# First feed-forward: its two square layers as seven products of quarters over two token blocks at a time

## The chip, the cores and the metric

The program runs on one core of one Trainium2 chip. The metric is the device time of one execution in microseconds. The kernel before took 2341.57 us, the median of three runs (2340.15 to 2347.95).

## The reference

Input is `x`, 4 sequences of 1024 tokens with 256 features, all in float32. Four parts follow one another, each behind a layer norm and added to `x`:

1. an attention with 8 heads of 64 and a latent of 64 for keys and values;
2. a feed-forward with ternary weights (-1, 0 or 1) and a scale per output:
```
h = silu(tlin(x, w1)) * tlin(x, w2)      # 256 -> 1024
h = gelu(tlin(h, h1))                    # 1024 -> 1024
h = gelu(tlin(h, h2))                    # 1024 -> 1024
y = tlin(h, w3)                          # 1024 -> 256;  tlin(x, w) = (x @ w.T) * s
```
3. an attention with 16 heads of 16 and rotated queries and keys;
4. a gated feed-forward of width 768 with integer weights.

The change is in part 2, and in what parts 1 and 3 do for it or beside it.

## The kernel before, in words

**Two programs.** `attention_a` is part 1, `ffn_attention_ffn` holds parts 2 to 4. Each engine has its own function (`sync`, `scalar`, `vector`, `gpsimd`, `tensor`), whose order is written out by hand: every engine walks the same numbered slots and does in each what the slot's functions name. Engines meet through semaphores alone, so an instruction that waits holds back all that its engine has behind it. All DMAs are issued by SyncE.

**Part 1.** A turn (`u, j`) is two steps of 128 keys for a pair of heads; there are 128 turns. TensorE makes scores, maxima twelve steps ahead, and weighted values; ScalarE the exponents (L631) and half of the maxima's work (L598); VectorE the other half (L785) and some sums of exponents (L803, L807); GpSimd the other sums (L952 to L959). Beside that, one weight tile of part 2 every four turns (`tile_at`, `load_tile` L523 to L529) is copied in DRAM to `wcopy`, loaded to `tile`, rounded by ScalarE (`tile_high`, L687) and compared by VectorE (L831). If no tile changes by the rounding, a flag lets the later program multiply rounded operands in one pass each (`exact`), with an activation as a high part and a low part that are multiplied one after the other.

**Part 2.** 4096 tokens are 8 blocks of 512 (`NB`). A block has 64 slots (`SLOTS`), and its 352 matmuls of 128x128 weights on 128x512 activations are spread over them, five or six in a slot (`slice_at`, `tile_of`): 64 for gate and up, 128 for each of the two square layers, 32 for down. An output tile of the square layers is 16 matmuls into one PSUM bank (8 inner pieces, high and low). Six banks go round (`Y`, `y_order`). Weights stream from `wcopy` through three buffers `wt`, one tile of 512 KB for 16 matmuls (L1594 to L1598). ScalarE applies Gelu twice per tile, once to the rounded high part and once to `xf` (L1874, L1875); GpSimd subtracts them to make the low part (`low`, L2070). For the gated layer ScalarE makes Silu, VectorE multiplies (`up`, L2012), ScalarE rounds (L1860), GpSimd subtracts.

**Side work.** One PSUM bank `X` serves, slot by slot (`x_at`), what stands beside the products. For block k it is done in the slots of block k+1: four transposes back with the residual (`BACK`), then the norm for part 3 on VectorE (`C_STATS` slot 15, `C_SCALE` slot 18, L184 to L206), two turns to feature order (`C_TURN` slots 22 and 24: TensorE transposes, ScalarE copies, VectorE subtracts, L227, L238, L249), four projections of queries and keys (`PROJECT`, each followed by three GpSimd operations of rotation, L2078 to L2082, and a low part, L2087) and four of values. The norm for the next block's gated layer (`B_STATS` to `B_TURN`) comes after. TensorE can begin a side operation only when the bank's user before it has been read out (`wait_free`). In the slots of each engine the side operation stands first, then the read-out of finished tiles, then the norm:

```
for H in range(END):
    if maximum_at(H) is not None: reduce(maximum_at(H))
    x = x_at(H) or ("",)
    ...                                  # turn, swap, residual
    for key in ended_at(H):
        if key[0] == "up": up(key)
    ...
    if norm_at(H): norm_step(*norm_at(H))
```

**Part 3** begins at slot `START` = 512 and has 512 half-steps. Each has one exponent of 128x1024 on ScalarE (L1813) and one maximum of 128x1024 on VectorE (L1965); the first 24 maxima stand in the last 24 slots of part 2. The side work of block 7 lies in its first 45 slots. Queries go through three tiles for units 2 to 4 (a unit is 16 half-steps) and four from unit 5. **Part 4** follows at slot 1024.

## Time and profile before

| what | value |
|---|---|
| median of three runs | 2341.57 us (2340.15 to 2347.95) |
| the profiled execution | 2332.85 us |
| its span, first to last instruction | 2331.0 us |
| granted TensorE clock, mean | 0.996 |
| part 1 | from 0 to about 720 us |
| part 2 | 722.6 to 1460 us |
| part 3 | 1461 to about 2192 us |
| part 4 | to the end |

Times come from one profiled execution. Matmuls overlap, so that the duration of one (0.39 us) is not what it adds: how far apart they start is. A group's "idle before" names the time its engine stood still in front of it and what ended that. The stages are read apart, since another engine can be the full one in each.

### The profile page before, as it was taken

What the parts mean: (1) busy time and instruction counts of PE and PEld (TensorE: products, weight loads), DVE (VectorE), ACT (ScalarE), POOL (GpSimd) and SP (SyncE); (2) the same over time, 40 slices, a digit from 0 to 9 for tenths busy, and PEclk for the clock granted to TensorE, in tenths of its full rate; (3) what the DMA queues carried; (4) which work ended last, traced back from release to release, by engine and by line L of the source; (5) the groups of instructions that cost most, each with busy time, mean ns of one, the idle gap of its engine ahead of it and who ended that gap; (6) DMA issues with size and microseconds to landing.
All of it is one profiled execution on the core that took longest, in us unless ns stands there. A gap on an engine that the chain in (4) does not pass through costs nothing.

```text
span 2331.0 us, 39372 instructions
## 1 busy us (share of the span) xinstructions
PE 2286.6 (98%) x14921; PEld 1414.8 (61%) x14921; DVE 1378.5 (59%) x2150; ACT 1463.2 (63%) x2049; POOL 1001.8 (43%) x646
## 2 busy tenths in 40 slices
PE   7999999999998999999999999999999999999999
PEld 5455555555556888888888886444444444444688
DVE  6655766666743143232232224889889889998364
ACT  5777777777764444444444443678777777778643
POOL 2676766757763373664655645120100000000354
PEclk9999999999999999999999999999999999999999
DMA  2213222222214455555555546343332332331232
GB/s 63 69 52 100 82 74 84 82 80 76 74 31 165 158 178 183 183 182 192 182 175 190 193 165 190 92 105 77 90 87 59 93 82 64 92 90 41 81 112 77
DMA packets 156841, 259.07 MB, mean 111 GB/s; under 512 B 37004, under 2 KB 97292, under 8 KB 156300
## 3 DMA queue, kind: packets, MB, share of 16 engines
q1 hardware_dynamic: 156652, 256.53, 36.6%
q8 instruction: 121, 1.98, 0.4%
q14 instruction: 68, 0.56, 0.1%
HBM read 206.52 MB, written 60.68 MB: 115 GB/s over the span
## 4 chain that ended last, share of the span: by engine, by line
PE 63%; ACT 2%; DVE 1%; issue 1%; DMA 1%; SPq 1%; POOL 0%; POOLq 0%
PE m_R L130 47%; PE m_O L130 11%; PE m_X L130 4%; ACT m_P L1813 1%; DMA m_K<-bounce_k 1%; PE m_X L227 1%; SPq L1671 0%; DVE m_mraw L1965 0%; ACT m_OS L1820 0%; PE m_X L2179 0%; DVE m_ln_x L206 0%; PE m_R L227 0%; DMA inverses<-m_rinv 0%; DVE m_ln_stat L184 0%; SPq L1698 0%
## 5 line engine op out<-in xcount | busy, mean ns | idle before, releaser
L1965 DVE TENSOR_REDUCE m_mraw<-m_R 128x2 f32<-128x1024 f32 x512 | 622.6, 1221 | 68.5 <-PE m_R L130 56.0
L1813 ACT ACTIVATE m_P<-m_R 128x1024 f32<-128x1024 f32 x512 | 523.7, 1025 | 148.6 <-PE m_R L130 148.3
L130 PE MATMUL m_O<-m_P,m_V 128*17 128x256 f32 x4096 | 329.4, 393 | 4.4 <-ACT m_P L1813 2.5
L785 DVE CUSTOM_DVE_ANT_0 a_excess<-a_X,a_excess 128x512 f32<-128x512 f32 x256 | 166.5, 688 | 170.6 <-PE a_X L130 167.9
L955 POOL TENSOR_TENSOR a_accp<-a_accp,a_P 128x1024 f32<-128x1024 f32 x96 | 253.9, 2645 | 24.5 <-ACT a_P L631 16.2
L631 ACT ACTIVATE a_P<-a_S 128x1024 f32<-128x1024 f32 x256 | 249.7, 1040 | 8.5 <-PE a_S L130 8.5
L2070 POOL TENSOR_TENSOR m_act0l<-m_xf,m_act0h 128x512 fp32r<-128x512 f32 x128 | 164.8, 1290 | 209.2 <-ACT m_xf L1875 110.9
L130 PE MATMUL m_R<-m_act0h,wt 128*128 128x512 f32 x640 | 251.4, 393 | 0.0
L130 PE MATMUL m_R<-m_act0l,wt 128*128 128x512 f32 x640 | 250.4, 391 | 0.0
L130 PE MATMUL a_O<-a_P,a_V 128*64 128x512 f32 x1024 | 247.7, 605 | 0.0
L130 PE MATMUL m_R<-m_Q,m_K 64*128 64x512 f32 x800 | 200.1, 497 | 2.3 <-DVE m_mraw L1965 2.0
L130 PE MATMUL m_R<-m_act1l,wt 128*128 128x512 f32 x512 | 202.0, 395 | 0.0
L130 PE MATMUL m_R<-m_act1h,wt 128*128 128x512 f32 x512 | 200.7, 392 | 0.0
L130 PE MATMUL m_R<-m_K,m_Q 48*128 48x512 f32 x800 | 181.7, 449 | 3.8 <-ACT m_P L1813 1.9
L2094 POOL TENSOR_TENSOR m_ON<-m_ON,m_yt 128x512 f32<-128x512 f32 x16 | 20.6, 1285 | 380.1 <-DMA m_yt<-inverses 380.1
L130 PE MATMUL m_R<-next_hi,wt 128*128 128x512 f32 x424 | 168.1, 396 | 2.8 <-PEq L40 2.8
L130 PEld LDWEIGHTS m_O<-m_P,m_V 128*17 128x17 f32 x4096 | 85.2, 120 | 139.3 <-issue 129.8
L130 PE MATMUL m_R<-next_lo,wt 128*128 128x512 f32 x424 | 167.7, 395 | 0.0
L130 PEld LDWEIGHTS m_R<-m_Q,m_K 64*128 64x128 f32 x800 | 74.5, 183 | 150.9 <-issue 126.0
L598 ACT ACTIVATE a_excess<-a_X 128x512 f32<-128x512 f32 x244 | 132.2, 596 | 36.3 <-PE a_X L130 35.5
L130 PEld LDWEIGHTS m_R<-m_act0h,wt 128*128 128x128 f32 x640 | 120.2, 188 | 26.9 <-POOL m_act0l L2070 2.1
L130 PEld LDWEIGHTS m_R<-m_act0l,wt 128*128 128x128 f32 x640 | 120.3, 188 | 24.5 <-issue 0.5
(274 smaller groups left out, 4130.1 us busy)
## 6 DMA issues: line engine op xcount, KB each, us to landing
wt<-wcopy SPq DMA_DIRECT2D x176, 512.0 KB, 3.3
m_K<-bounce_k SPq DMA_DIRECT2D x96, 128.0 KB, 5.5
m_ln_x<-x SPq DMA_DIRECT2D x23, 512.0 KB, 4.0
a_tile<-in_L_ffn_tiles SPq DMA_DIRECT2D x22, 512.0 KB, 3.6
wcopy<-in_L_ffn_tiles SPq DMA_DIRECT2D x22, 512.0 KB, 5.0
x<-xres SPq DMA_DIRECT2D x78, 128.0 KB, 1.7
m_Q<-bounce_q SPq DMA_DIRECT2D x150, 64.0 KB, 2.3
xres<-x SPq DMA_DIRECT2D x64, 128.0 KB, 2.7
```

Source lines behind the costliest of these rows:

```text
L130: return pe.eng.matmul(out, lhsT, rhs, start=start, stop=stop, skip_group_check=True)
L227: ins = pe.eng.transpose(bank[:, 128 * k:128 * k + 128], self.x[:, 4 * half + k, 128 * f:128 * f + 128], ident)
L598: act.eng.activation(excess[:, h, :], max_bank(n, h), ACT.Relu).then_inc(freed)
L631: act.eng.activation(P[n % NP][:, :, :], psS[n % 2][:, :, :], ACT.Exp, scale=SCALE).then_inc(s_exp)
L785: dve.eng.tensor_tensor_reduce(excess[:, h, :], bank(key), excess[:, h, :], 1.0, LOWEST, ALU.add, ALU.max, mraw[u % 2][:, q, h:h + 1]).the ...
L955: pool.eng.tensor_tensor(accp[:, :, :], accp[:, :, :], P[n % NP][:, :, :], ALU.add).then_inc(s_addp)
L1813: act.eng.activation(P[h % 4][:, :, :], pair(key)[:, :, :], ACT.Exp, scale=SCALE).then_inc(R.free(key))
L1965: dve.eng.tensor_reduce(mraw[u % 2][:, at, :], pair(key)[:, :, :], AX.X, ALU.max).then_inc(R.free(key))
L2070: pool.eng.tensor_tensor(act_buf[dst][1][:, m, :], xf[fs(key) % 2][:, :], f32(act_buf[dst][0][:, m, :]), ALU.subtract).then_inc(s_lo)
L2094: pool.eng.tensor_tensor(ON[:, f, cols], ON[:, f, cols], yt[half][:, :], ALU.mult).then_inc(s_norm[half])
```

## The change

**Two blocks at a time.** Blocks 2s and 2s+1 form a pair of 128 slots with five matmuls in each (`PACE`), 640 in all: 128 gate and up, 224 for each square layer, 64 down. Input features are halved (4 pieces of 128 each), output features are halved, and the two token blocks are the other halving, so that a layer is a 2x2 by 2x2 product of quarters, done by seven products (`m1` to `m7`) of 4 output tiles x 4 inner pieces x 2 parts. `m1` and `m2` share their banks, as do `m5` and `m3`.

**Sums of weights.** Four of the seven need sums of weight quarters. They are made in part 1, in four sets (`MIXES`) of 18 turns: the set's four quarter tiles are loaded and compared as before, then come four sums or differences of 128x1024 on VectorE and four stores of 512 KB to `wcopy` (now 38 tiles). The stores stand two turns behind the instructions that make their data. One quarter in four needs no copy in DRAM. The rounded tile for the comparison is int8.

**Sums of activations.** For every layer and each of 4 pieces VectorE makes four sums or differences of 128x512 in place (`mix`, each waiting for the one before), in slots 23, 25, 26 and 28 of the pair for the first square layer and 67, 69, 70 and 72 for the second. VectorE adds product to product (`leave`); ScalarE keeps `m1`, applies Gelu once per tile, and rounds 28 operands per layer and 16 for down (`high`); the low parts go to GpSimd and VectorE (`by_pool`).

**Side work** moves one block later: block k's lies in the slots of block k+2 (even: norm statistics in slot 21 and scaling in 24, turns in 28 and 30; odd: 15, 18, 22, 24 of the second 64). So part 3 now begins with the side work of blocks 6 and 7. The norm of block 1 is made in slots 2 to 9 of the first pair. The first 24 maxima go from slot 456 on, one in two slots, in one buffer. Queries have three tiles up to unit 8. Fills of `K1`, `Q2` and `V` go to GpSimd at slot 502.

```diff
-    NB, MT, PER, SLOTS = 8, HID0 // 128, 22, 64
+    NB, MT, PER, SLOTS, PACE = 8, HID0 // 128, 40, 64, 5
...
+    FIRST_MAX = START - 2 * ML - 8
...
-    BACK = (2, 4, 6, 8)
-    C_LOAD, C_STATS, C_SCALE, C_TURN = 10, 15, 18, (22, 24)
+    ORDER = ("m1", "m2", "m6", "m7", "m4", "m5", "m3")
+    OPERAND = dict(zip(ORDER, ("b11", "b21", "t2", "t3", "t4", "t1", "b22")))
...
+    BACK = (6, 8, 10, 12, 14, 16, 18, 20)
+    C_LOAD, C_STATS, C_SCALE, C_TURN = (16, 10), (21, 15), (24, 18), ((28, 30), (22, 24))
+    PROJECT = [{at + i: x for at, x in ((0, ("k", 0)), (4, ("q", 0)), (8, ("k", 1)), (12, ("q", 1)))} for i in (32, 26)]
...
+    N_LOAD, N_STATS, N_SCALE, N_TURN = 51, 56, 60, (2, 4)
+    ONE_STATS, ONE_SCALE, ONE_TURN = 2, 4, (7, 9)
...
-    QUERY_TILES = [0, 1, 2, 0, 1] + [(3, 2, 0, 1)[(u - 5) % 4] for u in range(5, NU)]
+    QUERY_TILES = [0, 1, 2] * 3 + [(3, 0, 1, 2)[(u - 9) % 4] for u in range(9, NU)]
...
+        layer, r = divmod(q - 128, 224)
+        if layer < 2:
+            return (ORDER[r // 32], 2 * s + layer, r // 8 % 4), r % 8, 8
+        return ("down", 2 * s + r // 32, r // 16 % 2), r % 16, 16
...
+            if l % 2:
+                H = (640 * (l // 2) + 128 + 192 + 8 * j + 7) // PACE + 2
+            else:
+                H = high_slot(("b22", l, j)) + 2
```
The new part of part 1 on SyncE and VectorE:
```diff
+                elif step == 12:
+                    sp.wait_ge(s_mix, 4 * n + 3)
+                    sp.eng.dma_start(sum_of(n, 0), f32(tile_hi[:, :])).then_inc(s_mixed, 16)
+                    sp.eng.dma_start(sum_of(n, 2), tile[:, :]).then_inc(s_mixed, 16)
+                    sp.eng.dma_start(sum_of(n, 1), third).then_inc(s_mixed, 16)
+                elif step == 13:
+                    sp.wait_ge(s_mixed, 64 * n + 48)
+                    sp.eng.dma_start(tile[:, :], wtiles[quarter(n, 0, 1)]).then_inc(s_tile, 16)
...
+                if i == 0:
+                    dve.eng.tensor_tensor(second, first, second, ALU.add).then_inc(s_mix)
```
And of part 2 on ScalarE, VectorE and GpSimd:
```diff
+            def keep_first(key):
...
+                act.eng.activation(kept[m], psY[Y.slot(("c11", l, m))][:, :], ACT.Copy).then_inc(s_kept)
...
+            def high(op):
+
+                act.wait_ge(*made(op))
+                if operand_free(op):
+                    act.wait_ge(*operand_free(op))
+                act.eng.activation(operand(op)[0], in_place(op), ACT.Copy).then_inc(s_hi)
...
+                elif name == "m7":
+                    dve.wait_ge(*Y.emptied(("m6", l, m)))
+                    dve.eng.tensor_tensor(kept[m], bank, twos[m], ALU.add).then_inc(Y.free(key))
...
+            def mix(l, j):
+
+                x11, x12, x21, x22 = [whole[place][j] for place in ("11", "12", "21", "22")]
+                n = 4 * mix_order[l, j]
+                dve.wait_ge(*(gelu_done(l - 1, "12", j) if l % 2 else up_done(l, "12", j)))
+                dve.wait_ge(*low_done(("b22", l, j)))
+                dve.eng.tensor_tensor(x22, x22, x12, ALU.subtract).then_inc(s_mixed)
+                dve.wait_ge(s_mixed, n + 1)
+                dve.wait_ge(*low_done(("b11", l, j)))
+                dve.eng.tensor_tensor(x12, x12, x11, ALU.subtract).then_inc(s_mixed)
+                dve.wait_ge(s_mixed, n + 2)
+                dve.eng.tensor_tensor(x11, x22, x11, ALU.add).then_inc(s_mixed)
+                dve.wait_ge(s_mixed, n + 3)
+                dve.wait_ge(*low_done(("b21", l, j)))
+                dve.eng.tensor_tensor(x21, x21, x11, ALU.subtract).then_inc(s_mixed)
...
+                for op in lows_at(H, False):
+                    low(op)
+                for l, j in mixes_at(H):
+                    mix(l, j)
...
+                pool.eng.tensor_tensor(lo, in_place(op), f32(hi), ALU.subtract).then_inc(s_lo[1])
```
On TensorE `m2` waits for `keep_first` of its tile and adds to that bank:
```diff
+                    if key[0] == "m2":
+                        pe.wait_ge(s_kept, 4 * key[1] + key[2] + 1)
+                    elif key[0] == "m3":
+                        pe.wait_ge(s_c22, 4 * key[1] + key[2] + 1)
```

## Rows read from the trace of the kernel before

**Rows 1.** Page of the profile, busy time by engine over the span
```profile
PE 2286.6 (98%) x14921; PEld 1414.8 (61%) x14921; DVE 1378.5 (59%) x2150; ACT 1463.2 (63%) x2049; POOL 1001.8 (43%) x646
```

**Rows 2.** Stretches (start:end, length, busy us and count by engine): feed-forward, second attention, one block
```profile
722.60:1460.40 737.80, 737.25 (x3371) 598.68 (x3371) 219.41 (x399) 331.99 (x534) 403.36 (x318) 1.00 0.56 181
1461.00:2192.00 731.00, 719.30 (x6395) 308.58 (x6394) 632.03 (x636) 565.10 (x629) 66.18 (x64) 1.00 0.32 79
971.29:1062.56 91.27, 91.27 (x426) 75.62 (x425) 24.65 (x50) 42.18 (x69) 53.20 (x42) 1.00 0.57 184
```

**Rows 3.** Chain that ended last inside the feed-forward (880 to 1336 us): start, us, what
```profile
by line: PE m_R L130 88.1%; PE m_X L130 9.1%; PE m_X L227 1.8%; PE m_X L2179 1.0%
...
971.29 19.98 PE m_R L130 x88
```

**Rows 4.** Groups by line in the feed-forward stage (722 to 1460 us)
```profile
L130 PE MATMUL m_R<-m_act0h,wt 128*128 128x512 f32 x640 | 251.4, 393 | 0.0
...
L2070 POOL TENSOR_TENSOR m_act0l<-m_xf,m_act0h 128x512 fp32r<-128x512 f32 x128 | 164.8, 1290 | 209.2 <-ACT m_xf L1875 110.9 <-ACT m_act0h L1860 98.3
...
L1875 ACT ACTIVATE m_xf<-m_R,scol 128x512 f32<-128x512 f32 x128 | 87.3, 682 | 0.0
...
L1860 ACT ACTIVATE m_act0h<-m_xf 128x512 fp32r<-128x512 f32 x64 | 39.9, 623 | 4.3 <-DVE m_xf L2012 4.3
...
L2012 DVE SCALAR_TENSOR_TENSOR m_xf<-m_R,scol,m_P 128x512 f32<-128x512 f32 x32 | 24.0, 751 | 23.0 <-PE m_R L130 22.1
...
L249 DVE TENSOR_TENSOR next_lo<-m_X,next_hi 128x512 fp32r<-128x512 f32 x28 | 19.4, 692 | 149.6 <-ACT next_hi L238 149.6
```

**Rows 5.** Timeline of VectorE around one normalisation (start, us, instruction)
```profile
941.79 1.39 DVE L184 BATCH_NORM_STATS2 m_ln_stat<-m_ln_x 128x6 f32<-128x256 f32 x4
943.21 0.38 DVE L187 BATCH_NORM_AGGREGATE m_ln_mv<-m_ln_stat 128x2 f32<-128x6 f32 x4
943.63 0.85 DVE L192 TENSOR_SCALAR m_ln_ve<-m_ln_mv 128x4 f32<-128x4 f32 x1
...
949.33 5.27 DVE L206 TENSOR_SCALAR m_ln_x<-m_ln_x,m_ln_mv,m_ln_rstd 128x256 f32<-128x256 f32 x4 [0.34 <-POOL m_ln_rstd L201]
```

**Rows 6.** Timeline of VectorE, 740 to 749 us: differences of two SBUF tiles
```profile
741.10 1.45 DVE L1989 TENSOR_TENSOR m_wql<-m_P,m_wqh 128x512 fp32r<-128x512 f32 x1 [1.22 <-ACT m_wqh L1898]
742.47 0.68 DVE L1989 TENSOR_TENSOR m_wkl<-m_P,m_wkh 128x512 fp32r<-128x512 f32 x1
```

**Rows 7.** Line 206 over the whole span: ns min/median/max
```profile
L206 DVE TENSOR_SCALAR m_ln_x<-m_ln_x,m_ln_mv,m_ln_rstd x92: 397/412/1391, 768.3 to 2296.2; 128x256 f32<-128x256 f32 x92
```

**Rows 8.** Groups of VectorE in the first attention (0 to 722 us)
```profile
L803 DVE TENSOR_TENSOR a_accd<-a_P 128x1024 f32<-128x1024 f32 x32 | 61.8, 1931 | 0.4
L831 DVE SCALAR_TENSOR_TENSOR a_tile_hi<-a_tile,a_tile_hi 128x1024 f32<-128x1024 f32 x27 | 56.9, 2109 | 0.0
```

**Rows 9.** Line 803, the same operation, ns min/median/max
```profile
L803 DVE TENSOR_TENSOR a_accd<-a_P x32: 1172/1858/3161, 49.6 to 696.8; 128x1024 f32<-128x1024 f32 x32
```

**Rows 10.** Exponents of the first attention (line 631) between 100 and 600 us
```profile
100.00:600.00 500.00, 183.33 (x188) 1.00 0.24 79
```

**Rows 11.** Page, DMA issues: KB each, us to landing
```profile
m_ln_x<-x SPq DMA_DIRECT2D x23, 512.0 KB, 4.0
...
wcopy<-in_L_ffn_tiles SPq DMA_DIRECT2D x22, 512.0 KB, 5.0
```

**Rows 12.** SyncE's queue at the start of the feed-forward
```profile
722.38 0.38 SPq L177 DMA_DIRECT2D m_ln_x<-x  x1
```

**Rows 13.** Exponents of the second attention (line 1813) in stretches of 20 us
```profile
1500.00:1520.00 20.00, 9.56 (x10) 1.00 0.42 87
1520.00:1540.00 20.00, 12.08 (x13) 1.00 0.49 142
1540.00:1560.00 20.00, 15.43 (x16) 1.00 0.19 57
```

**Rows 14.** Line 1965, maxima of the second attention, ns min/median/max
```profile
L1965 DVE TENSOR_REDUCE m_mraw<-m_R x512: 1155/1225/1230, 1414.6 to 2148.9; 128x2 f32<-128x1024 f32 x171
```

More of the change, by code:

```diff
@@ L9 @@
 I32 = mybir.dt.int32
+I8 = mybir.dt.int8
 ALU = mybir.AluOpType
@@ new lines, in high_slot @@
+    def high_slot(op):
+        name, l, j = op
+        if name[0] == "d":
+            l = 2 * l + 2
+        began = 640 * (l // 2) + 128 + 224 * (l % 2)
+        before = began - 224 if l % 2 else 640 * (l // 2 - 1) + 352
+        if l % 2 == 0 and name in ("b11", "b21", "b22"):
+            up = 640 * (l // 2) + 8 * (j + 1) + {"b11": 0, "b21": 32, "b22": 96}[name]
+            return (up - 1) // PACE + 1
+        if name == "t2":
+            return (before + 224) // PACE + 1 + j if l % 2 else began // PACE + 2 + j
+        if name in ("t3", "t4", "t1"):
+            return (began + {"t3": 34, "t4": 66, "t1": 98}[name] + 8 * j) // PACE + 1
+        if name == "d12":
+            return (before + 224) // PACE + 1 + j // 2
+        return (before + {"11": (130 + 8 * j), "21": (162 + 8 * j), "22": (194 + 6 * j)}[name[1:]]) // PACE + 1
@@ new lines, in ffn_attention_ffn, with by_pool @@
+    operands = [(name, l, j) for l in range(2 * B) for name in OPERAND.values() for j in range(4)]
+    operands += [(name, s, j) for s in range(B) for name in ("d11", "d21", "d22", "d12") for j in range(4)]
+    highs = {}
+    for op in operands:
+        highs.setdefault(high_slot(op), []).append(op)
+    high_order = {op: i for i, op in enumerate(op for H in sorted(highs) for op in highs[H])}
+    def by_pool(op):
+        return op[0] in ("b11", "b21", "d11", "d21") or op[2] % 2 == 1
+    low_order = {op: sum(by_pool(x) == by_pool(op) and high_order[x] < i for x in operands) for op, i in high_order.items()}
@@ new lines, in done, with operand @@
+        def done(key):
+            if key[0] in ("m1", "m5"):
+                return (s_m1 if key[0] == "m1" else s_m5), 4 * key[1] + key[2] + 1
+            return Y.filled(bank_of(key))
+        def last_of(i):
+            s, q = divmod(i, PER)
+            return tile_of(s, 16 * q + 15)[0]
+        def operand(op):
+            name, l, j = op
+            slot = {"b11": 0, "t3": 0, "d11": 0, "b21": 1, "t4": 1, "d21": 1, "b22": 2 + l % 2, "t2": 3 - l % 2, "t1": 3 - l % 2, "d22": 2, "d12": 3}[name]
+            return slots[slot][:, j, :], slots[slot][:, 4 + j, :]
@@ L1862, in leave @@
+            def keep_first(key):
+                _, l, m = key
+                act.wait_ge(*done(key))
+                if l:
+                    act.wait_ge(s_c22, 4 * (l - 1) + m + 1)
+                if l % 2 == 0 and m == 3:
+                    act.wait_ge(*Y.emptied(("up", l + 1, MT - 1)))
+                act.eng.activation(kept[m], psY[Y.slot(("c11", l, m))][:, :], ACT.Copy).then_inc(s_kept)
             def leave(key):
-                bank = psY[Y.slot(key)]
-                act.wait_ge(*Y.filled(key))
@@ L2015, in last_up, with low @@
+            def low(op):
+                dve.wait_ge(*high_done(op))
+                hi, lo = operand(op)
+                dve.eng.tensor_tensor(lo, in_place(op), f32(hi), ALU.subtract).then_inc(s_lo[0])
             def last_up(k, m):
@@ L2052, in vector @@
                     norm_step(*norm_at(H))
-                if H in C_PIECES:
-                    norm_piece(norm_of["c", NB - 1], C_PIECES.index(H))
+                for half in range(2):
+                    if H in C_PIECES[half]:
+                        norm_piece(norm_of["c", NB - 2 + half], C_PIECES[half].index(H))
                 if H in D_PIECES:
@@ L2114, in gpsimd @@
             for H in range(END):
-                if H == START + 48:
+                if H == START + 112:
                     fill_queries()
-                for key in ended_at(H - 1):
-                    if key[0] == "up":
-                        low(key)
+                for op in lows_at(H, True):
+                    low(op)
+                if H == START - 10:
+                    for i in range(5):
+                        fill_late(i)
                 if send_high_at(H):
@@ L2139, in gpsimd @@
                     norm.power(pool, norm_at(H)[0])
-                if H == C_PIECES[1]:
-                    norm.power(pool, norm_of["c", NB - 1])
+                for half in range(2):
+                    if H == C_PIECES[half][1]:
+                        norm.power(pool, norm_of["c", NB - 2 + half])
                 if H == D_PIECES[1]:
@@ L2167, in product @@
                 if not exact:
                     lhsT, rhs = f32(lhsT), f32(rhs)
-                ins = mm(pe, psY[Y.slot(key)][:, :], lhsT, rhs, at == 0, at == n - 1)
+                ins = mm(pe, psY[Y.slot(bank)][:, :], lhsT, rhs, at == 0 and key[0] not in ("m2", "m3"), at == n - 1)
                 if at == n - 1:
-                    ins.then_inc(Y.full(key))
+                    ins.then_inc(done(key)[0])
             def back(key):
@@ L2373, in weight_tiles @@
     tiles = [np.stack([w[:, :, 256 * q:256 * q + 256] for w in rows[:2]], 1) for q in range(4)]
-    tiles += [w[:, :, 128 * m:128 * m + 128] for w in rows[2:] for m in range(w.shape[2] // 128)]
+    tiles += [w[:, 4 * col:4 * col + 4, 512 * row + 256 * half:512 * row + 256 * half + 256]
+              for w in rows[2:4] for row in range(2) for col in range(2) for half in range(2)]
+    tiles += [rows[4][:, :, 128 * m:128 * m + 128] for m in range(2)]
     return np.ascontiguousarray(np.stack([t.reshape(128, 1024) for t in tiles]).astype(np.float32))
```

527 lines of the change are left out of this document (372 added, 155 removed).

## The prediction

> **What bounds the kernel now.** I read the stretches first. TensorE is busy for 98% of the span [rows 1], but a matmul's duration overlaps with the next, so the stages have to be read one by one. In the first feed-forward it is busy for 737.25 of 737.80 us, VectorE for 30%, ScalarE for 45%, GpSimd for 55% [rows 2]; the chain of waits there consists of TensorE alone [rows 3]. That stage is bound by the number of matmuls. What one costs is not its 393 ns [rows 4] but its distance to the next: 88 in 19.98 us, 0.227 us each [rows 3]. A block takes 91.3 us [rows 2]; its 352 products are 79.9 of them, side work 11.4. In the second attention VectorE's maximum takes 1.225 us [rows 14] of a half-step of 1.25 us (16 in 20 us [rows 13]), so two engines are nearly full there.
>
> **The saving.** 704 products for two blocks become 640: 4 x 64 = 256 fewer, times 0.227 us, **-58.1 us**. Weight tiles fall from 44 to 40 per pair, one per 16 products as before. A slot is now 5 x 0.227 = 1.135 us.
>
> **What the other engines take on, per pair of 128 slots** (168 us, from 2 x 91.3 less 64 x 0.227). ScalarE loses 64 Gelus and 16 roundings [rows 4] and gets 8 copies, 32 Gelus and 72 roundings: 84 becomes about 99 us. VectorE gets 40 read-outs and 24 low parts at 0.69 and 32 differences at 0.68 [rows 4, 6]: 50 becomes about 116. GpSimd keeps 48 low parts of 1.29 beside the rotations: 106 as before [rows 2, 4]. All three fit on average, so by shares this costs nothing. What can cost is the order on VectorE, where 16 differences per layer stand close together, each behind the one before.
>
> **The even chain (first square layer).** Let 0 be TensorE's start of slot 21. VectorE has the statistics of the side block's norm: 1.39 + 0.38 + about 0.7 us [rows 5]. It gets to them at 0.95, behind the read-out of a tile, and is through at 3.45. Then in program order: two multiplications of 0.75 [rows 4] and one low part of 0.65 (5.5), the differences of piece 0, four dependent ones of 0.72 (0.68 [rows 6] and 0.04 between dependent ones), 2.9 us (8.4), the scaling of the norm, 4 x 0.41 without GpSimd [rows 7] (10.0), a multiplication and a low part (11.3), pieces 1 and 2 (17.1), the first turn's read-out (17.8), a low part, piece 3 (21.3), the second turn's read-out (22.0). TensorE has slots of its own pace: it is at slot 28 at 8.0 and needs the scaled norm of 10.1 (waits 2.1); at slot 30 it is there at 12.9 and needs the single bank X, free at 17.8 (waits 4.9); at slot 32 it needs the second turn at 22.0 (waits 1.3). Together 8.3 us. Nothing covers this: side operations stand in TensorE's own order, and behind them queue the products. It happens in pairs 1 to 3 (pair 0 has no side block yet). Before, VectorE was busy for only 24.65 us of a block's 91.27 [rows 2].
>
> GpSimd adds to it. A subtraction of two SBUF tiles took 1.45 us instead of 0.68 [rows 6] when it met a GpSimd operation, and four scalings 5.27 instead of 1.65 [rows 5, 7]. Three GpSimd low parts (b22 of pieces 1 and 3, t2 of piece 1) fall into this stretch; at most 1.29 each, that is 0 to 3.9. I take 1.2, for a **9.5 us** each: **+28.5** (bounds 20 and 37).
>
> **The odd chain (second square layer).** No side operation stands in slots 67 to 85, but ScalarE's order does harm: it rounds t2 of piece 3 in slot 74, which needs VectorE's last differences, and only behind it keeps tiles 2 and 3 of `m1`, which `m2` needs. From the start of slot 65: VectorE reads out four tiles, makes low parts and has the last t2 at 17.1, ScalarE has tile 2 kept at 18.5, TensorE wants it at 75 x 0.227 = 17.0. That is 1.5 us, up to 5.4 with three GpSimd operations; I take 3 in three pairs. In the last pair the maxima begin at slot 72 of it, with one buffer: the second one waits for VectorE's first reduction of 1.225 [rows 14], which stands in the same crowd (about 15.5 against 10.7); there I take 6. **+15** (6 to 30). Pair 0's even chain has the same order on ScalarE: **+1** (0 to 4).
>
> **The start.** Block 1's norm is now needed in slot 7. Its load is issued at 722.38 [rows 12] and lands 4.0 us later [rows 11]; statistics, power, scaling (2.5 + 1 + 1.65, and two multiplications between) end at about 734, TensorE is there at about 732: **+2** (0 to 4).
>
> **Rotations.** GpSimd makes three rotations and a low part of 1.29 per projection, 5.2 us, and up to two more low parts in four slots (4 x 1.135 + side 2.2 = 6.7 us). A lag of 2 us is covered by the distance between projections. **+0** (0 to 5).
>
> **Second attention.** The side work of one more block goes there. In the stage of before, two stretches with it have 23 half-steps in 40 us, which at 1.25 is 11.2 us too long [rows 13]; the feed-forward gives back 11.4 less the two turns of the next block, 10.7. With queries in three tiles for four more units: **+1.5** (0 to 6).
>
> **First attention.** A turn is 2 x 500/188 = 5.3 us [rows 10]. VectorE gets 16 sums of 128x1024, 1.17 to 3.2 us each, 1.86 typically [rows 9], in turns where it is 64% busy: 3.4 + 1.9 fills the turn. The comparisons (2.1 us each [rows 8]) stay 27, closer together. Maxima run 12 steps ahead and cover most: **+2.5** (0 to 20). On SyncE four copies go and 16 stores come. The wait of step 13 is for three stores of 512 KB, 5.3 us after their issue; a copy of that size landed in 5.0 alone [rows 11], so it may hold the queue for some 3 us, and behind it stand the moves of the maxima's rows and of inverses, which are needed a turn later or more: 0.
>
> **The sum:** -58.1 + 28.5 + 15 + 1 + 2 + 0 + 1.5 + 2.5 = -7.6 us on a profiled execution of 2332.85. The median of the runs lies 8.7 us above that one; I subtract from the median: 2334.0 us. A change within 0.3% (7.0 us) can hardly be told from none.
>
> The Trainium skill, SBUF — State Buffer, section "SBUF: two separate sides", says that VectorE operations with two SBUF inputs and GpSimd operations lock one port pair for a whole instruction, and that the loser is fully blocked. The trace agrees so far as the 1.45 us go; by this rule alone the time would be that of the second rival below.
>
> **Rivals.**
> - *VectorE keeps pace* (18%). If the differences run at their 0.6 us distance and TensorE's waits stay at 10 us for all eight chains, -58 + 10 + 6 gives 2299. For it: VectorE at 116 of 168 us. Against: the order above; 8.3 us need no contention.
> - *Slower: the port* (28%). Every GpSimd low part holds a difference for its 1.29. The even chains then cost 8.3 + 3.9 = 12.2 each, the odd ones 5.4, the last of these 9, pair 0 5, rotations 5, and the rest 6: 36.6 + 16.2 + 9 + 5 + 5 + 6 = 78, that is +20, 2361. It decides from where the eight chains, rotations with them, cost more than 52 us; mine are 44.5. The four scalings of 5.27 speak for it, the quiet of GpSimd in slots 21 to 31 (no projection) against.
> - *First attention bound by VectorE* (8%): all 16 sums on its path, 16 x 1.86 = 30 instead of 2.5, +20: 2361 too, but elsewhere.
> - *It doesn't do what it says* (4%): the feed-forward isn't shorter because weights arrive late or the flag falls the other way.
> - *The forecast*: 42%, its own range 2320 to 2348.
>
> Faster by over 0.3%: 18, about 25 of the forecast's 42 and 1 of the last. Within 0.3%: 12 of the forecast, 4 of the port, 2 of the others. The rest, 38, is slower. The range reaches from the pace rival to beyond the port: 2298 to 2368.
>
> **What would show it.** Matmuls on `wt` 256 fewer, at the same 0.227 us. In pairs 1 to 3 a hole of TensorE before the turns of slots 28 and 30, ended by VectorE's scaling and by its read-out, with a chain of differences in front; small holes before `m2` in the second layer, ended by ScalarE's copies. Differences of 0.68 or of 1.4 us tell forecast from port. Exponents of the first attention still 188 in 500 us. I am wrong if TensorE's holes in the feed-forward sum to under 20 us or over 75, or if part 1 moves by over 8 us.

## The result, and the profile after

The changed kernel took 2381.85 us (median of three runs, 2378.20 to 2387.66) against 2341.57: **1.0186 of the time before, 95% interval 1.0163 to 1.0208**. Forecast were 2334.0 us and a range of 2298 to 2368; the result lies above it. The profiled execution took 2378.2 us, its span is 2376.4 (before 2331.0), a difference of 45.4 us. The page's busy times, as in [rows 1]:

```profile
PE 2260.2 (95%) x14665; PEld 1377.3 (58%) x14665; DVE 1665.4 (70%) x2545; ACT 1513.2 (64%) x2169; POOL 1034.1 (44%) x651
```

The 256 matmuls are gone (14921 less 14665), yet TensorE's busy time fell by only 26.4 us where the forecast's saving is 58.1, and the span grew. The stretches, with the columns of [rows 2] (length, busy time and count of PE, PEld, DVE, ACT, POOL, granted clock, DMA share, GB/s), the feed-forward first:

```profile
727.00:1471.00 744.00, 687.28 (x3049) 552.05 (x3049) 478.38 (x751) 375.42 (x640) 407.34 (x306) 0.97 0.49 159
1471.00:2238.50 767.50, 743.90 (x6464) 317.69 (x6464) 640.49 (x663) 573.02 (x644) 88.21 (x81) 0.98 0.34 84
```

Part 1 ends 4.4 us later (722.6 to 727.0), the feed-forward takes 744.0 instead of 737.8 us, the second attention 767.5 instead of 732.2 (up to a point 12.7 us behind the first product of the last part, in both kernels), the rest 0.5 less: 4.4 + 6.2 + 35.3 - 0.5 = 45.4.

**The feed-forward.** TensorE's holes sum to 59.5 us between 727 and 1459, 3.3 before. Those of TensorE's timeline that carry the sum (start, us, instruction, and in brackets the idle time ahead of it and what ended it); the third pair of even and odd layers repeats the second:

```profile
739.04 0.66 PE L228 MATMUL m_X<-ident,m_ln_x 128*128 128x128 f32 x4 [2.17 <-DVE m_ln_x L207]
...
828.72 5.52 PE L131 MATMUL m_R<-m_act0l,wt 128*128 128x512 f32 x16 [2.97 <-ACT m_V L2152]
...
924.92 0.32 PE L228 MATMUL m_X<-ident,m_ln_x 128*128 128x128 f32 x1 [3.12 <-DVE m_ln_x L207]
934.16 1.11 PE L228 MATMUL m_X<-ident,m_ln_x 128*128 128x128 f32 x4 [4.72 <-DVE next_lo L250]
...
1006.20 5.54 PE L131 MATMUL m_R<-m_act0l,wt 128*128 128x512 f32 x16 [2.95 <-ACT m_V L2152]
...
1063.27 2.08 PE L131 MATMUL m_R<-m_act0h,wt 128*128 128x512 f32 x8 [3.13 <-issue]
1114.29 0.63 PE L228 MATMUL m_X<-ident,m_ln_x 128*128 128x128 f32 x4 [1.47 <-DVE m_ln_x L207]
1123.53 1.12 PE L228 MATMUL m_X<-ident,m_ln_x 128*128 128x128 f32 x4 [6.33 <-DVE next_lo L250]
...
1374.26 0.93 PE L131 MATMUL m_R<-m_act0h,wt 128*128 128x512 f32 x3 [1.76 <-DVE m_P L2344]
1378.79 4.15 PE L131 MATMUL m_R<-m_act0h,wt 128*128 128x512 f32 x10 [2.01 <-DVE m_P L2344]
```

In front of the even wait VectorE works without a pause. From its timeline, pair 2 (L2352 to L2360 are the four differences of a piece, L2319 the gated product, L2366 a low part, L250 a turn's read-out):

```profile
1105.42 1.39 DVE L185 BATCH_NORM_STATS2 m_ln_stat<-m_ln_x 128x6 f32<-128x256 f32 x4
...
1109.27 1.40 DVE L2352 TENSOR_TENSOR m_P<-m_P 128x512 f32<-128x512 f32 x1
1110.71 0.69 DVE L2355 TENSOR_TENSOR m_P<-m_P,m_whole 128x512 f32<-128x512 f32 x1
...
1112.77 1.37 DVE L207 TENSOR_SCALAR m_ln_x<-m_ln_x,m_ln_mv,m_ln_rstd 128x256 f32<-128x256 f32 x4
...
1116.04 1.67 DVE L2355 TENSOR_TENSOR m_P<-m_P,m_whole 128x512 f32<-128x512 f32 x1
...
1122.80 0.68 DVE L250 TENSOR_TENSOR next_lo<-m_X,next_hi 128x512 fp32r<-128x512 f32 x1
...
1126.77 0.68 DVE L250 TENSOR_TENSOR next_lo<-m_X,next_hi 128x512 fp32r<-128x512 f32 x1
```

The 1.67 us at 1116.04 is a difference that met a low part of GpSimd, which was running since 1115.55:

```profile
1115.55 1.61 POOL L2430 TENSOR_TENSOR m_act1h<-m_P,m_act1h 128x512 fp32r<-128x512 f32 x1 [5.42 <-ACT m_act1h L2142]
1119.17 1.71 POOL L2430 TENSOR_TENSOR m_act1l<-m_whole,m_act1l 128x512 fp32r<-128x512 f32 x1 [2.01 <-ACT m_act1l L2142]
```

It is so in all eight crowds of 16 differences: three GpSimd low parts begin beside each crowd, each of the 24 meets a difference, and these 24 take 1.40 to 1.67 us, where a difference that meets none takes 0.68 or 0.69.

**The clock.** Behind many of these holes the matmuls are further apart. The windows view shows the granted clock there; 0.5 is the lower of its two levels, 1.2 GHz (the last row belongs to the second attention):

```profile
931.70:938.50 6.80, 4.34 (x13) 3.57 (x14) 6.63 (x11) 2.45 (x4) 1.00 (x1) 0.51 0.00 0
1006.80:1010.20 3.40, 3.40 (x10) 2.67 (x9) 2.39 (x9) 2.84 (x6) 0.67 (x1) 0.53 0.02 5
...
1696.30:1706.50 10.20, 10.03 (x59) 3.22 (x59) 5.40 (x6) 4.47 (x6) 0.73 (x1) 0.51 0.25 70
```

In the feed-forward there are nine such stretches after its first hole, 40.8 us in all, in the second attention five with 23.8 us. Before, the clock was at 2.4 GHz through both stages but for 3.4 us at their very start. What it cost can be read off TensorE's busy time: 256 products and 10.7 us of side work less should have taken 68.8 us from the 737.25 of [rows 2]; busy time fell by 50.0, to 687.28. So the same matmuls took **18.8 us** longer. With the holes the stage comes out: -68.8 + 18.8 + 56.2 = +6.2.

Not all of the 18.8 us is the clock. In the three even chains the clock fell while TensorE was still waiting, so that of the 40.8 us at 1.2 GHz TensorE was busy for 31.4; half of that, 15.7 us, is what the lower clock cost. The other 3 us are about what the waits leave in the busy time: the last matmul in front of a wait runs out its 0.39 us where the next would have started after 0.227, and there are some two dozen waits of over 0.3 us (an estimate: 26 x 0.16 = 4.2).

The Trainium skill, "TensorE: Matmul & The Clock Gate", section "What's actually happening", says that the array's clock is gated down to half when TensorE has lately been idle. These rows agree. The forecast had no term for it.

**The second attention.** ScalarE's exponents (L2094) in stretches of 20 us from its start, as [rows 13]:

```profile
1470.00:1490.00 20.00, 10.14 (x10) 0.87 0.83 217
1490.00:1510.00 20.00, 13.11 (x13) 0.96 0.44 133
1510.00:1530.00 20.00, 10.47 (x11) 0.91 0.21 45
1530.00:1550.00 20.00, 10.15 (x10) 1.00 0.43 89
1550.00:1570.00 20.00, 12.28 (x13) 1.00 0.52 166
1570.00:1590.00 20.00, 15.40 (x16) 1.00 0.41 89
...
1610.00:1630.00 20.00, 10.85 (x11) 1.00 0.07 21
1630.00:1650.00 20.00, 9.90 (x10) 1.00 0.64 140
...
1690.00:1710.00 20.00, 8.54 (x9) 0.74 0.50 104
```

A count takes in instructions cut by the border, so I go by busy time: one exponent is 1.025 us, and 15.43 us in 20 of a stretch without side work [rows 13] are 15.05 half-steps, **1.33 us** each (the forecast took 1.25). Before, the slow stretch is 80 us long and not 40:

```profile
1460.00:1540.00 80.00, 48.24 (x48) 1.00 0.37 105
1540.00:1620.00 80.00, 61.81 (x61) 1.00 0.35 76
```

The first 142 half-steps took 206 us before (from the first exponent at 1461.1 to 1667.3) and 237 after (1472.4 to 1709.4), 31 more. Taken by units of 16 exponents, from the start of one unit to the start of the next, the growth has four places (us):

| unit | 0 | 1 | 2 | 3 | 4 | 5 | 6 | 7 | 8 | 24 |
|---|---|---|---|---|---|---|---|---|---|---|
| before | 22.2 | 28.7 | 28.7 | 21.3 | 21.2 | 21.2 | 21.3 | 21.2 | 23.2 | 22.1 |
| after | 27.7 | 27.5 | 32.9 | 21.4 | 21.2 | 28.7 | 28.7 | 21.3 | 30.2 | 25.2 |

A unit without side work takes 21.2 us. The turns, projections and values of the further block stand in units 5 and 6 and cost 15 us. Units 0 to 2 are 8.5 longer; before as after they hold one block's side work, now with the transposes back of both blocks, and three stretches at 1.2 GHz (10.2 us) and more waits lie there. Unit 8 is 7.0 longer: the wait of 3.98 us for keys and the 10.2 us at 1.2 GHz behind it. Unit 24 is 3.1 longer: another wait for keys, 1.55 us, and 3.4 us at 1.2 GHz. Together 33.6 of the 34.6 us by which the 512 exponents took longer.

This stage differs from one execution to the next. In the runs below that leave its code as it is (2, 5 and 6) its length is 762 to 773 us where it was 767.5 here, and for the old kernel's code (runs 7 and 8) 736 and 740 where it was 732.2. So its 35.3 us of growth are certain to some 5 only.

### The profile page after: what moved, and what is told of

Read it like the earlier page. It is cut to its first block, busy times and chain, and to the rows that moved or that the text cites. A ratio compares the mean times of both kernels' runs of the same rounds, so it can differ in the third digit from the quotient of the medians.

```text
span 2376.4 us, 39311 instructions
## 1 busy us (share of the span) xinstructions
PE 2260.2 (95%) x14665; PEld 1377.3 (58%) x14665; DVE 1665.4 (70%) x2545; ACT 1513.2 (64%) x2169; POOL 1034.1 (44%) x651
## 4 chain that ended last, share of the span: by engine, by line
PE 52%; DVE 8%; issue 3%; DMA 3%; ACT 2%; SPq 2%; POOL 0%; DVEq 0%; ACTq 0%; POOLq 0%
PE m_R L131 37%; PE m_O L131 10%; PE m_X L131 4%; DVE m_P L2355 1%; DMA m_K<-bounce_k 1%; DVE m_ln_x L207 1%; DVE m_P L2352 1%; DVE m_whole L2357 1%; SPq L1942 1%; ACT m_P L2094 1%; DMA xres<-x 1%; DVE m_mraw L2272 1%; PE m_X L228 1%; ACT m_OS L2101 0%; DVE m_ln_stat L185 0%
## 5 line engine op out<-in xcount | busy, mean ns | idle before, releaser
L2094 ACT ACTIVATE m_P<-m_R 128x1024 f32<-128x1024 f32 x512 | 523.7, 1025 | 163.4 <-PE m_R L131 162.8
L131 PE MATMUL m_R<-m_Q,m_K 64*128 64x512 f32 x832 | 210.8, 503 | 6.2 <-DVE m_mraw L2272 5.4
L131 PE MATMUL m_R<-m_K,m_Q 48*128 48x512 f32 x832 | 191.1, 455 | 12.5 <-DMA m_K<-bounce_k 6.0
L131 PE MATMUL m_R<-m_act1l,wt 128*128 128x512 f32 x704 | 171.2, 393 | 4.5 <-issue 3.7
L131 PE MATMUL m_R<-m_act0h,wt 128*128 128x512 f32 x576 | 147.9, 409 | 9.9 <-issue 6.1
L131 PE MATMUL m_R<-m_act0l,wt 128*128 128x512 f32 x576 | 145.7, 402 | 11.1 <-ACT m_V L2152 11.1
L131 PEld LDWEIGHTS m_R<-m_act1l,wt 128*128 128x128 f32 x704 | 130.1, 188 | 33.1 <-issue 5.6
L131 PEld LDWEIGHTS m_R<-m_act0l,wt 128*128 128x128 f32 x576 | 110.5, 195 | 37.2 <-ACT m_V L2152 13.2
L202 POOL TENSOR_TENSOR m_ln_rstd<-m_ln_ve,m_ln_minus_half 128x4 f32<-128x4 f32 x23 | 23.3, 1014 | 244.8 <-DVE m_ln_ve L193 244.8
L131 PEld LDWEIGHTS a_O<-a_P,a_V 128*64 128x64 f32 x1024 | 62.2, 136 | 108.7 <-issue 106.2
L131 PE MATMUL m_R<-next_hi,wt 128*128 128x512 f32 x296 | 118.6, 401 | 2.8 <-PEq L41 2.8
```

Of the source, the lines that this page charges most:

```text
L131: return pe.eng.matmul(out, lhsT, rhs, start=start, stop=stop, skip_group_check=True)
L2094: act.eng.activation(P[h % 4][:, :, :], pair(key)[:, :, :], ACT.Exp, scale=SCALE).then_inc(R.free(key))
```

## The experiments

Thirteen kernels ran. What the expectations call A is this: the waits behind VectorE's crowd of differences, and the lower clock behind them, ate the saving. B is the rival that each text names. Ratios are to the kernel before, with their 95% interval; the changed kernel's is 1.0186.

**1. The even turns later**

```diff
-    ..., C_TURN = (16, 10), (21, 15), (24, 18), ((28, 30), (22, 24))
+    ..., C_TURN = (16, 10), (21, 15), (24, 18), ((34, 36), (22, 24))
```
(projections from 38, values from 40, the rope's load at slot 60)

> The changed kernel with the even block's turns in slots 34 and 36 instead of 28 and 30 and its projections six slots later, behind the crowd of differences. Theory A (TensorE waits for VectorE's chain in pairs 1 to 3, 7.8 us each, and the granted clock falls to 1.2 GHz behind such waits, 23.8 us of it here, which costs 0.47 of that time): the three pairs of waits go and the clock stays up there, 23.5 + 11 us less, 2347 us, ratio to the kernel before 1.0025. Theory B (the low clock has nothing to do with the waits): 23.5 us less, 2358 us, ratio 1.007, and the stretches at 1.2 GHz remain.

Measured 1.0174 [1.0154, 1.0193]. The waits moved: 2.41 us before `m2` at 1122, 5.04 before the turn at 1129, 56.4 us between 720 and 1460 in all. Neither expectation (1.0025 and 1.007) came; six slots' delay bought nothing that can be told from noise.

**2. t2 rounded later**

```diff
-  return (before + 224) // PACE + 1 + j if l % 2 else began // PACE + 2 + j
+  return (before + 224) // PACE + 1 + (0, 1, 4, 6)[j] if l % 2 else began // PACE + 2 + (0, 1, 3, 5)[j]
```

> The changed kernel with ScalarE's rounding of t2 of pieces 2 and 3 moved behind the copies of m1 (slots 75 and 77, and 30 and 32). A: the waits of m2 for ScalarE's copy (2.97 us three times, 2.2 in pair 0) go with the three stretches at 1.2 GHz of 3.4 us behind them: 11 + 5 us less, 2366 us, ratio 1.010. B: 11 us less, 2371 us, ratio 1.0125. Rival C (ScalarE's order was not the cause, the copy waits for something else): no change, 1.0186.

Measured 1.0211 [1.0192, 1.0230]. The waits before `m2` are gone, so ScalarE's rounding of t2 in front of the kept tiles was their cause, as forecast. But the time that should have gone with them did not. In their place the odd turns wait 4.84 and 4.85 us for the scaled norm; holes 58.9 us.

**3. Both**

> Both moves together. A: 34.5 + 16 us less, 2331 us, ratio 0.996. B: 34.6 us less, 2347 us, ratio 1.0025. If holes only move elsewhere (the engines can't keep pace at all): over 1.012.

Measured 1.0165 [1.0142, 1.0188]. One even wait in each pair where there were two: 8.66, 7.75 and 7.63 us; holes 55.0 us. In pair 2 VectorE is busy in front of it without a pause for 22.5 us. Moved by six slots, the turn still meets a VectorE that is not through.

**4. The last part's weights loaded later**

```diff
-                if H == START + 122:
+                if H == START + 150:
                     load_last_back()
```

> The changed kernel with the load of part 4's last weights (three transfers) at half-step 150 of the second attention instead of 122, where it stands right ahead of the keys' fetch. A: the wait of 3.98 us for the keys and the 10.2 us at 1.2 GHz behind it go, 8.5 us less, 2373 us, ratio 1.015. B: 4 us less, 2378 us, ratio 1.017. Rival: the keys are late because the fetch itself is issued late; no change.

Measured 1.0184 [1.0159, 1.0208]. The wait for keys at 1698 fell from 3.98 to 1.12 us and the 10.2 us at 1.2 GHz behind it went; unit 8 took 23.3 us, as in the kernel before. A residual's wait of 2.83 us (1.72 in the changed kernel) with 10.2 us at 1.2 GHz stands at 1490. In the total nothing was gained.

**5. Differences of activations on 8 columns** (of 512: the sums of activations are left out)

```diff
-                x11, x12, x21, x22 = [whole[place][j] for place in ...]
+                x11, x12, x21, x22 = [whole[place][j][:, 0:8] for place in ...]
```

> The changed kernel with the 16 differences per layer made on 8 of 512 columns, so VectorE's chain between up and the low parts is shorter by 16 x 0.6 us per layer (the sums of activations are left out, all else is as in the changed kernel). Theory A (the length of VectorE's chain makes TensorE's waits, and the low clock follows them): waits in the feed-forward fall from 56 to under 15 us, the stretches at 1.2 GHz behind them go, 40 + 15 us less, 2327 us on the first chip, ratio 0.994. Theory B (waits cost only themselves): 40 us less, ratio 1.001. Theory C (port and queues rather than the chain's length): waits stay above 35 us, ratio over 1.010.

Measured 0.9974 [0.9959, 0.9989]. The stretches:

```profile
727.70:1425.00 697.30, 675.55 (x3049) 544.29 (x3049) 409.68 (x751) 375.97 (x640) 403.57 (x306) 0.99 0.52 169
1425.00:2197.70 772.70, 744.05 (x6463) 318.60 (x6463) 640.34 (x663) 573.09 (x644) 88.17 (x81) 0.98 0.35 84
```

The feed-forward falls from 744.0 to 697.3 us with the same matmuls: 35 us of idle time and 11.7 of busy time go. So VectorE's 128 differences cost the feed-forward 46.7 us, by their waits and the clock behind them; that is more than the 40 by which the changed kernel was slower. The total lies between the expectations of A (0.994) and B (1.001): 21.7 us of holes stayed, where A said under 15, among them two of 3.15 and 3.20 us marked "issue", with the lower clock at their end. The run takes the crowd's length and its meetings with GpSimd out together, so it does not part the two. The second attention stays long (772.7).

**6. The weights' sums in part 1 on 8 columns** (of 1024: most of each sum is left out)

```diff
-                first, second = tile[:, :], f32(tile_hi[:, :])
+                first, second, last = tile[:, 0:8], f32(tile_hi[:, 0:8]), third[:, 0:8]
```

> The changed kernel with the sums of weights in the first attention made on 8 of 1024 columns (they are left out; loads, stores and comparisons stay). What the 16 sums cost on the path: the first attention shrinks by 2 to 4 us of the 4.4 it grew, ratio 1.017. If the moves are to blame instead, no change, 1.0186. If VectorE bounds the first attention, more than 8 us.

Measured 1.0190 [1.0152, 1.0227]. The feed-forward began at 724.31, and at 727.0 to 729.3 in the kernels with full sums: the sums make 2.7 us of part 1's 4.4, or somewhat more; in the total it can't be told.

**7 and 8. A wait put into the kernel before.** Before the first turn's read-out of blocks 0 to 6, four (then nine) more reductions on VectorE, with the old number of matmuls:

```diff
+                    if NORMS[x[1]][0] == "c" and NORMS[x[1]][1] < NB - 1 and x[2] == 0:
+                        for _ in range(4):
+                            dve.eng.tensor_reduce(pad[:, 0:1], psX[0][:, :], AX.X, ALU.max).then_inc(s_pad)
```

> The kernel before, with four extra reductions of about 0.7 us on VectorE between a block's first turn and its read-out, in 7 blocks. TensorE should wait about 2 us seven times. A and B: 14 us more, ratio 1.006, if waits this short leave the clock up; if they too bring it down, 1.2 GHz for 3.4 us each, 11 us more: 1.011.

Measured 1.0051 [1.0035, 1.0068], 2350.64 against 2338.73 us. The median rose by 11.9 us (8 to 16 by the interval). Seven waits of 1.70 us are 11.9 together, and that the two agree to the tenth is luck; the clock stays at 1.00 behind each:

```profile
933.83 0.66 PE L227 MATMUL m_X<-ident,m_ln_x 128*128 128x128 f32 x4 [1.70 <-DVE next_lo L249]
```
```profile
839.60:846.40 6.80, 6.55 (x31) 5.51 (x32) 1.64 (x4) 2.36 (x4) 1.63 (x3) 1.00 0.40 122
```

> As e7_dose4 with nine reductions: TensorE should wait 5.5 us seven times. A: each wait is followed by 3.4 to 6.8 us at 1.2 GHz, half of which is lost: 38 + 11 to 22 us more, ratio 1.021 to 1.026. B: 38 us more, ratio 1.0165, clock 0.996 as before.

Measured 1.0221 [1.0197, 1.0244], 2391.23 us: +52.5 (46 to 57 by the interval). Seven waits of 5.33 us are 37.3. Around each the clock stands at half, for 6.8 us in six cases and 3.4 in one. In the six it fell 2.4 to 3.1 us before the wait ended, in the one as it ended; TensorE was busy at the lower clock for 3.4 to 4.5 us in all seven (the last row is the one of 3.4):

```profile
942.16 1.12 PE L227 MATMUL m_X<-ident,m_ln_x 128*128 128x128 f32 x4 [5.33 <-DVE next_lo L249]
```
```profile
839.60:846.40 6.80, 3.58 (x11) 3.00 (x12) 3.76 (x6) 0.60 (x1) 0.00 (x0) 0.51 0.15 41
1136.50:1143.40 6.90, 4.15 (x12) 3.48 (x13) 3.32 (x5) 0.60 (x1) 0.00 (x0) 0.51 0.22 62
942.00:945.40 3.40, 3.24 (x10) 2.76 (x11) 0.80 (x2) 0.60 (x1) 0.00 (x0) 0.52 0.22 37
```

The feed-forward of this trace takes 789.6 us instead of 737.8, 51.8 more. Of these 37.3 are the waits, and half of the 28.0 us for which TensorE was busy at the lower clock is 14.0: together 51.3. Short waits cost their length, long ones 1.4 times theirs. This is the cleanest measurement of the term that the forecast lacked, since only the number of reductions differs between runs 7 and 8.

**9. The even norm behind the differences**

```diff
-    ... (16, 10), (21, 15), (24, 18), ((28, 30), (22, 24))
+    ... (16, 10), (30, 15), (33, 18), ((36, 38), (22, 24))
```

> The changed kernel with the side block's norm of even halves placed wholly behind the crowd of differences: statistics in slot 30 (was 21), scaling in 33 (was 24), turns in 36 and 38 (were 28 and 30), projections and values 8 slots later than they were. Nothing is taken out. Theory A: the even waits are there because VectorE has statistics, scaling and a turn's read-out inside the 21.5 us that the differences take; behind them it has idle time again, so the waits of 7.8 us in pairs 1 to 3 and the 23.8 us at 1.2 GHz behind them (some 12 lost) go: holes of TensorE in the feed-forward fall from 59 to 33 to 38, the ratio to the kernel before falls from 1.0186 to 1.003 to 1.008. Theory B: as in the three reorderings before, the holes only move (to the turns at 36 and 38, or to the kept tiles): 55 us or more, and 1.016 to 1.020.

Measured 1.0232 [1.0207, 1.0257]: worse than both expectations. The even waits became one of 8.77 us each, for the scaling. I had placed the norm by slots, as if VectorE reached slot 30 when TensorE does.

**10. That, with all other moves**

```diff
-    ... (30, 15), (33, 18), ((36, 38), (22, 24))
+    ... (30, 19), (33, 22), ((36, 38), (26, 28))
```
(and t2 as in 2, the last weights as in 4, residuals five slots ahead instead of three)

> All that the runs so far point to, nothing taken out: even norms behind the differences (as in the run of the norm alone), the rounding of t2 spread over more slots (odd layers 0, 1, 4, 6 and even layers 0, 1, 3, 5), the odd halves' norm four slots later (statistics 19, scaling 22, turns 26 and 28), the weights of the last part loaded at half-step 150 of the second attention instead of 122, residuals loaded five slots ahead instead of three. Theory A: holes of the feed-forward fall to 15 to 25, stretches at 1.2 GHz there to under 10 us, and the residual's wait in the second attention goes: 0.992 to 1.001 of the kernel before. Theory B (the holes move): 1.014 to 1.020. If the second attention stays 30 us longer than before with its waits gone, its growth is work and not waits: then 0.997 to 1.003.

Measured 1.0122 [1.0104, 1.0140], between A and B. The odd waits before `m2` are gone (2.82 and 2.87 us for the scaled norm stand in their place); even waits of 9.8 us remained, and 58 us of holes in all, so that A's "15 to 25" did not come. VectorE's timeline shows why:

```profile
1112.57 0.69 DVE L2360 TENSOR_TENSOR m_whole<-m_whole 128x512 f32<-128x512 f32 x1
1113.18 1.40 DVE L185 BATCH_NORM_STATS2 m_ln_stat<-m_ln_x 128x6 f32<-128x256 f32 x4
...
1116.69 3.26 DVE L207 TENSOR_SCALAR m_ln_x<-m_ln_x,m_ln_mv,m_ln_rstd 128x256 f32<-128x256 f32 x4 [0.90 <-POOL m_ln_rstd L202]
```

The last difference ends at 1113.3, the statistics of "slot 30" follow, and TensorE has been at slot 36 since 1110.3 (its turn began at 1120.10 behind 9.81 us).

**11. Only the second attention's loads moved** (last weights at 150, residuals five ahead)

> The changed kernel with only the loads of the second attention moved: the weights of the last part at half-step 150 instead of 122, residuals five slots ahead instead of three; the feed-forward keeps its order but for the residual loads. If waits on these loads, and the 1.2 GHz behind them, make 5 to 10 of the 35 us that the second attention grew, the ratio falls to 1.014 to 1.016 and the residual's wait of 1.7 to 5.6 us near half-step 20 is gone. If the 35 us are work of a further block on the two engines, the ratio stays at 1.017 to 1.020.

Measured 1.0161 [1.0137, 1.0186], at the border of the two expectations; 1.69 us of the residual's wait stayed. The stage took 759 us, 3 less than the shortest of those with its code unchanged. The loads are at most a small part of its growth.

**12. The even norm and its turns ahead of the differences, projections behind them**

```diff
-    C_LOAD, C_STATS, C_SCALE, C_TURN = (16, 10), (21, 15), (24, 18), ((28, 30), (22, 24))
+    C_LOAD, C_STATS, C_SCALE, C_TURN = (10, 10, 16, 10), (15, 19), (17, 22), ((19, 21), (28, 30), (28, 30), (22, 24))
-    BACK = (6, 8, 10, 12, 14, 16, 18, 20)
+    BACK = ((1, 3, 5, 7, 10, 12, 14, 16), (6, 8, 10, 12, 14, 16, 18, 20))
```
(the last two or the second entries are those of part 3, which keeps its slots; projections from 40 and 32, values from 42 and 34)

> The profile of the run before this one showed why its norm was still late: VectorE is through with the differences only 20 us after slot 26, so statistics in slot 30 are made at 1115 us, and TensorE is at the turn of slot 36 at 1110. Here the even halves' norm and both turns stand ahead of the crowd (residuals in slots 1 to 16, statistics 15, scaling 17, turns 19 and 21), the projections behind it (40 to 52, values 42 to 54); odd halves: statistics 19, scaling 22, turns 28 and 30, the next block's turns 48 and 50; rope loaded one half later, first keys and queries fetched 13 to 18 slots earlier, and the other moves of the run with all of them (t2 spread, weights of the last part at half-step 150, residuals five slots ahead). Theory A (waits and the clock they bring down are what ate the saving): the even waits of 9.8 us and the 10.2 us at 1.2 GHz behind each of them go, holes of the feed-forward under 20 us, ratio 0.990 to 0.998. Theory B (the crowd of differences holds TensorE up wherever the side work stands): the projections at 40 or the products m6 wait instead, 40 us of holes or more, 1.008 or more.

Measured **1.0036 [1.0019, 1.0054]**, all arithmetic in place. The holes that are left in pair 2, and the two stages (727.4 us is the feed-forward's start; the second row runs from ScalarE's table load ahead of the exponents):

```profile
1092.09 0.63 PE L228 MATMUL m_X<-ident,m_ln_x 128*128 128x128 f32 x4 [1.78 <-DVE m_ln_x L207]
1123.07 0.39 PE L131 MATMUL m_X<-m_wvh,next_hi 128*128 128x256 f32 x1 [1.42 <-DVE m_t L2288]
...
1240.29 3.36 PE L131 MATMUL m_R<-m_act1l,wt 128*128 128x512 f32 x8 [4.11 <-issue]
```
```profile
727.40:1436.00 708.60, 669.31 (x2995) 533.70 (x2996) 478.98 (x748) 366.42 (x631) 399.44 (x300) 0.99 0.51 164
1436.00:2204.90 768.90, 750.65 (x6519) 326.99 (x6518) 642.50 (x666) 577.07 (x654) 96.68 (x88) 0.99 0.36 86
```

In the same bounds the feed-forward was 732.0 us in the changed kernel and 730.5 before. 35 us of the total came back through order alone; stretches at 1.2 GHz within the feed-forward fell from 40.8 to 13.6 us. Run 10 had the other moves already and stood at 1.0122; between the two lie the even norm and its residuals ahead of the crowd, small shifts of the odd turns and of the next block's norm, and earlier first fetches. The even wait of 9.8 us became two of 1.78 and 1.42. The expected 0.990 to 0.998 was missed, since 41.5 us of holes remain and the second attention did not shorten by more than 10.6 us (779.5 to 768.9; before 739.6).

**13. Sends one slot later, first maxima six slots later**

```diff
-        return x_of(H - 6, "project")
+        return x_of(H - 7, "project")
-    FIRST_MAX = START - 2 * ML - 8
+    FIRST_MAX = START - 2 * ML - 2
```

> The run before this one (norms ahead of the crowd) left in the feed-forward two waits of 3.4 and 4.1 us for weights, whose loads stood on the queue behind a send that waits for GpSimd, each with 3.4 us at 1.2 GHz behind it, and 5.4 us where the maxima begin within the last pair's differences, with 6.8 us at 1.2 GHz. Here each send stands one slot later and the first 24 maxima begin six slots later. If these waits can be had (they and their clock are some 20 us), 8 to 15 us go and the ratio falls from 1.0036 to 0.997 to 1.001. If they only move, 1.002 to 1.006. The second attention, 27 us longer than before in half-steps lost beside side work, should stay as it is: so no order of the feed-forward alone should bring 0.990.

Measured 1.0039 [1.0025, 1.0053], no different from run 12. That is what the expectation said for waits that only move. The waits for weights fell to 1.23 and 1.77 us and the feed-forward to 702.0, but the second attention took 772.6; a wait of 3.70 us at 1612 is new there, ended by an exponent. No version with all its arithmetic in place beat the kernel before.

## Why the prediction was wrong

**The step that failed** is that every wait of TensorE was priced at its own length, and that the waits were looked for in the feed-forward alone. What the runs showed in its place:

- A long wait brings the lower clock with it. In the feed-forward the matmuls took 18.8 us longer than their number asks for, 15.7 of it by the lower clock. Runs 7 and 8 show the term by itself: 11.9 us of waits in pieces of 1.70 cost 11.9, 37.3 us in pieces of 5.33 cost 52.5.
- By size the largest miss is the second attention: 24.6 us net (35.3 in the stage, less the 10.7 given back) where **1.5** was forecast. Its side work was mis-sized by little: 12.2 us was taken for the block in the stage, and units 5 and 6 show 15. The other 20 us are waits and stretches at 1.2 GHz, for which the forecast had no term there: 23.8 us at 1.2 GHz, in which TensorE was busy throughout, so at most 12 us of cost; and 23.6 us of holes where 11.7 were before. 15, 12 and 12 are more than 35.3, so the three overlap. The split is worked out from the traces, and how much each is worth stays open: no run took the side work out of this stage.

The single steps:

- **The saving.** Right: 256 matmuls fewer at 0.227 us where the clock is full.
- **The even chain**, 9.5 us in each of three pairs: measured 7.8 (3.12 + 4.72, 1.47 + 6.33, 1.48 + 6.34). The mechanism and its place were right; the third wait of 1.3 us, at slot 32, did not come. For GpSimd 1.2 us was taken; the three meetings held VectorE for some 2.6. That the sum came near is two errors against each other.
- **The odd chain**, 3 us each: measured 2.97, 2.95, 2.97; run 2 shows the cause. The last pair, 6: measured 6.3. Pair 0's even chain, 1: 0.97 + 1.27. The start, 2: 2.17.
- **Rotations, 0**: wrong in its form. GpSimd's rotation and low part hold SyncE's send of a projection, and weight loads queue behind it (SyncE's own waits, 727 to 1471: us in total, times, longest):

```profile
SPq L1919 <- POOL m_comp L2465: 84.3, 21, 7.3
```

  Holes of 3.13, 3.00, 1.74, 1.04 and 0.92 us marked "issue", and two of 1.28 for `m_t`, are 12.4 us. In front of the one at 1063.27 a send left SyncE at 1057.44, as soon as GpSimd's low part was done, and two weight loads behind it at 1057.86. The forecast asked what TensorE waits for on GpSimd, not what is queued behind the send on SyncE. Run 13 moved the sends and the maxima, and these waits shrank.
- **Holes in all**: the named terms foresaw 46.5 us in the feed-forward, 56.2 more than before came. That is 10 us of the miss.
- **Second attention**, the step "23 half-steps in 40 us, at 1.25": the half-step is 1.33, and the 23 are 21.1 by busy time. These two slips cancel: 40 less 21.1 x 1.33 is 12. What was left out is the other two of the four slow stretches of 20 us.
- **First attention, 2.5**: 4.4, of which 2.7 or somewhat more is the sums (run 6).
- **ScalarE's load** per pair comes to 102 us by the forecast's own rows and not to 99; nothing hangs on it.

The terms in a row: forecast -7.6, measured +45.4 on the profiled executions, 53.0 apart: longer matmuls in the feed-forward 18.8, holes there 9.7, second attention 33.8, first 1.9, the last part -0.5, together 63.7. Against that stand 10.7 us of side work, which the forecast had set off in the term of the second attention and which show here in the feed-forward: 63.7 - 10.7 = 53.0.

The rivals: *VectorE keeps pace* was out from the first hole. *The port* was right in its sign and nearer in its time (2361), and its meetings all came, 24 of 24. But each held a difference for 0.7 to 1.0 us and not 1.29, and the even chains cost 7.8 and not 12.2, so the time above the forecast did not come from there. The Trainium skill, "SBUF — State Buffer", section "SBUF: two separate sides", says that the one of the two that starts first keeps the shared ports for its whole instruction while the other is blocked; the 24 meetings agree with it. *First attention bound by VectorE* was wrong (4.4 us). The forecast's limit "wrong if the holes sum to over 75" was not reached, and the result was wrong all the same: in the feed-forward it named holes as the only thing that could go wrong.

## What to carry to other kernels

When TensorE is the engine that bounds a stage, ask of each new wait how long it is in one piece: here waits of 1.7 us cost their length and waits of 5.3 us 1.4 times it, through the clock. An engine that is idle a third of the time can still set the pace if a dependent crowd of work stands in its program order ahead of what the full engine asks for next; moving the asking by a few slots moves the wait, and only putting the asked-for work ahead of the crowd (run 12) took most of it away. Side work that is pushed into the next stage must be priced by what it costs there, read over the whole of the stretch that it fills, and with the waits that it brings.

## What was not expected of the hardware

The lower clock does not follow a wait's length alone. Waits of 2.95 to 2.97 us before `m2` were each followed by 3.4 us at 1.2 GHz, one of 3.13 us at 1063.27 was not, and one of 3.00 at 1252.08 was. In run 1 the first of the waits before `m2`, again 2.96 us and at the same place of the program (829.75), was not followed by it. In the second attention a wait of 3.98 us for keys was followed by 10.2 us at 1.2 GHz. Of seven equal waits of 5.33 us six had 6.8 us around their end and one 3.4, though the time for which TensorE worked at the lower clock differed by 1.1 us only. What decides between these no run here shows.
